# Chunked cross-attention on one core: softmax and value product in pieces of 512 tokens instead of 256, transposed squares placed by transfer alone

## The reference

```python
q, k, v = (ctx.transpose(0, 2, 1) @ W.T + b for W, b in ...)      # three 256 -> 256 projections of ctx
# tokens fall into chunks of 64; 8 heads of 32 channels
scores = einsum('bnqhd,bnkhd->bnhqk', q, k) / sqrt(32)            # 64 x 64 for each chunk and head
scores = scores + where(mask_of_key > 0, 0, -1e9)
out = einsum('bnhqk,bnkhd->bnqhd', softmax(scores), v)
out = (out @ W_out.T + b_out).transpose(0, 2, 1) * mask + x
return (out - mean(out, axis=2)) * rsqrt(var(out, axis=2) + 1e-5) # over the 2048 tokens of each channel
```

## Time and profile before

| | |
|---|---|
| median of 3 runs | 2021.92 us |
| the profiled execution: its own time / its span | 2024.09 / 2022.3 us |
| busy PE, PE weight loads, DVE, ACT, POOL | 97%, 79%, 87%, 77%, 74% of the span |
| share of PE in the chain that ended last | 96% |
| granted TensorE clock | 0.992 (mean; 1 is 2.4 GHz, 0.5 is 1.2 GHz) |

### The profile page before, as it was taken

How to read it: one execution, slowest core, us unless ns; L and a number is a source line. 1 busy time by engine, 2 the same in 40 slices (tenths; PEclk the granted TensorE clock), 3 DMA queues, 4 the chain that set the end, 5 groups by cost and what they waited for, 6 DMA issues and landing times.

```text
span 2022.3 us, 91553 instructions
## 1 busy us (share of the span) xinstructions
PE 1967.5 (97%) x40472; PEld 1597.4 (79%) x40472; DVE 1764.8 (87%) x2217; ACT 1565.7 (77%) x2176; POOL 1489.3 (74%) x1059
## 2 busy tenths in 40 slices
PE   7999999999999999999999999999999999999995
PEld 6888888777778888888878888888878778788883
DVE  5888988888888898888989889898889888888886
ACT  5778778777778877878777787777878778877773
POOL 4677777867777777777777777777776777777774
PEclk9999999999999999999999999999999999999997
DMA  4455666556665566665556666566655566655654
GB/s 157 128 160 174 169 187 181 166 147 169 181 179 165 161 173 181 186 180 168 163 173 184 172 177 173 165 171 187 180 163 160 171 177 177 170 172 165 173 147 146
DMA packets 242890, 342.55 MB, mean 169 GB/s; under 512 B 28992, under 2 KB 94784, under 8 KB 242496
## 3 DMA queue, kind: packets, MB, share of 16 engines
q1 hardware_dynamic: 242496, 336.71, 57.8%
HBM read 168.82 MB, written 67.11 MB: 117 GB/s over the span
## 4 chain that ended last, share of the span: by engine, by line
PE 96%; issue 2%; DVE 1%; POOL 0%; DMA 0%; ACT 0%; SPq 0%; DVEq 0%; POOLq 0%; ACTq 0%
PE proj_bank L308 38%; PE proj_bank L342 19%; PE proj_bank L365 18%; PE score_bank L383 11%; PE o_bank L416 10%; DMA b_cols<-b_in 0%; POOL y L590 0%; DVE row_max L658 0%; DVE stats L709 0%; DVE y L700 0%; POOL prob L572 0%; DVE w_lo L641 0%; DVE y L736 0%; DVE o_lo L689 0%; DVE prob L662 0%
## 5 line engine op out<-in xcount | busy, mean ns | idle before, releaser
L572 POOL TENSOR_TENSOR prob<-prob,recip 128x1024 f32<-128x1024 f32 x256 | 487.4, 1904 | 498.6 <-DVE recip L673 498.6
L658 DVE TENSOR_REDUCE row_max<-score_bank 128x16 f32<-128x1024 f32 x256 | 313.5, 1225 | 185.5 <-PE score_bank L383 181.8
L474 ACT ACTIVATE prob<-prob 128x1024 f32<-128x1024 f32 x256 | 271.6, 1061 | 235.2 <-DVE prob L662 235.2
L308 PE MATMUL proj_bank<-ctx_hi,w_hi 128*128 128x512 f32 x1024 | 349.2, 422 | 12.6 <-DVE ctx_lo L644 9.2
L580 POOL TENSOR_TENSOR ctx_lo<-ctx_raw,ctx_hi 128x512 fp32r<-128x512 f32 x255 | 329.6, 1293 | 18.2 <-ACT ctx_hi L454 18.2
L590 POOL TENSOR_TENSOR y<-y,x_raw 128x512 f32<-128x512 f32 x256 | 325.9, 1294 | 7.6 <-DVE y L700 7.5
L308 PE MATMUL proj_bank<-ctx_lo,w_hi 128*128 128x512 f32 x1024 | 322.6, 396 | 0.3 <-issue 0.3
L308 PE MATMUL proj_bank<-ctx_hi,w_lo 128*128 128x512 f32 x1024 | 319.9, 393 | 1.3 <-issue 1.3
L662 DVE TENSOR_TENSOR prob<-score_bank,row_max 128x1024 f32<-128x1024 f32 x256 | 313.4, 1224 | 8.8
L681 DVE STREAM_TRANSPOSE squares<-prob 128x1024 f32<-128x1024 f32 x256 | 315.8, 1234 | 1.5 <-POOL prob L572 1.5
L669 DVE TENSOR_REDUCE sums<-prob 128x16 f32<-128x1024 f32 x256 | 304.9, 1191 | 1.2 <-ACT prob L474 1.1
(11 more groups left out here) (46 smaller groups left out, 3691.9 us busy)
## 6 DMA issues: line engine op xcount, KB each, us to landing
ctx_raw<-ctx SPq DMA_DIRECT2D x128, 512.0 KB, 5.8
x_raw<-x SPq DMA_DIRECT2D x128, 512.0 KB
prob_t<-squares SPq DMA_DIRECT2D x1024, 64.0 KB, 2.5
out<-y SPq DMA_DIRECT2D x128, 512.0 KB, 6.9
mask_all<-mask SPq DMA_DIRECT2D x128, 256.0 KB, 4.2
v_x<-v_f SPq DMA_DIRECT2D x256, 128.0 KB, 3.5
y<-w_in_t SPq DMA_DIRECT2D x1, 768.0 KB, 5.7
y<-w_out_t SPq DMA_DIRECT2D x1, 256.0 KB, 6.7
```

Of the source, the lines that this page charges most:

```text
L308: last = pe.matmul(proj_bank[:, f, :], w[:, h, col + f * P:col + (f + 1) * P], c[:, n % 2, h, :], start=(a == 0 and h == 0), stop=(a == 2 ...
L572: pool.tensor_tensor(part, part, slots(recip[:, u % 2, :]), ALU.mult).then_inc(norm_done, 1)
L658: dve.tensor_reduce(row_max[:, :].rearrange("p (r c) -> p r c", c=CPU), rows, AX_X, ALU.max).then_inc(max_done, 1)
```

## The change

Every engine now walks over **periods** `p` of a whole block instead of units: `periods(step)` with `p` from -3 to 131. Scores, maximum, subtraction, transposition, `high_attention`, `low_attention` and value product handle 512 tokens in one piece. Exponentials, sums, division and `lay_negatives` are made in two instructions per block, split by heads (`half`), each as large as one of a unit before. `copy_squares` is gone; `move_probs` transfers all eight squares of a block. `squares` and `prob_t` have one buffer of double size. The masks have a ring of six. `rstd` and `shift` have two buffers.

The orders by period (PE, SP, DVE, ACT, POOL):

```diff
+            def step(p):                      # tensor
+                scores(p + 1)
+                project_k(p + 2, 0); project_k(p + 2, 1)
+                project_q(p + 2, 0); project_q(p + 2, 1)
+                project_out(p - 2, 0)
+                probs_times_v(p - 1)
+                project_out(p - 2, 1)
+                project_v(p + 2, 0); project_v(p + 2, 1)
+            def step(p):                      # sync
+                load_mask(p + 3); load_ctx(p + 6); load_x(p - 1)
+                move_values(p + 1); move_probs(p); store(p - 7)
+            def step(p):                      # vector
+                less_maximum(p + 1); turn(p); statistics(p - 3)
+                if done: mean_and_variance((p - 3) // BLOCKS)
+                output(p - 2, 0); sum_up(p + 1, 0)
+                output(p - 2, 1); sum_up(p + 1, 1)
+                reciprocals(p + 1); low_attention(p - 1)
+                if done: mean_shift((p - 3) // BLOCKS)
+            def step(p):                      # scalar
+                keys(p + 2, 0); split_ctx(p + 3, 0); keys(p + 2, 1); split_ctx(p + 3, 1)
+                queries(p + 2, 0); queries(p + 2, 1)
+                exponentials(p + 1, 0); exponentials(p + 1, 1)
+                lay_negatives(p + 2, 0); lay_negatives(p + 2, 1)
+                high_attention(p - 1)
+                values(p + 2, 0); normalise(p - 7); values(p + 2, 1)
+            def step(p):                      # gpsimd
+                low_ctx(p + 3, 0); low_ctx(p + 3, 1); masked_keys(p + 2)
+                normalise(p - 7); [reciprocal_std]
+                add_residual(p - 2, 0); add_residual(p - 2, 1)
+                divide(p + 1, 0); divide(p + 1, 1)
```

(The diff writes each call on a line of its own.) The core of the parts that changed inside:

```diff
             def move_probs(n):
+                sp.wait_ge(turned, n + 1)
+                wait(sp, pv_done, n)
                 for f in range(HALVES):
                     for a in range(2):
-                        b = 1 - a
+                        for b in range(2):
-                        sp.dma_start(prob_t[target, u % 2, a, :, :],
-                                     squares[source, u % 2, b, :, :]).then_inc(moved[u], 16)
+                            sp.dma_start(prob_t[target, a, :, :],
+                                         squares[source, b, :, :]).then_inc(moved[n % MOVES], 16)
...
             def turn(n):
                 dve.wait_ge(norm_done, 2 * (n + 1))
+                if there(n - 1):
+                    dve.wait_ge(moved[(n - 1) % MOVES], 128 * ((n - 1) // MOVES + 1))
...
             def project_v(n, f):
+                if there(n - 4):
+                    pe.wait_ge(y_done, 2 * (n - 4) + f + 1)
...
             def project_out(m, f):
+                if there(m + 4):
+                    pe.wait_ge(q_f_done, 2 * (m + 4) + f + 1)
```

More of the change, by code:

```diff
@@ L23 @@
 CPU = UNIT // CHUNK
+CPB = BLOCK // CHUNK
+ALL = BATCHES * BLOCKS
+MASKS = 6
+MOVES = 8
 SQ = 32
@@ L26 @@
 TPU = UNIT // P
[L27 removed]
+SLOTS = ROWS * CPB
 EPS = 1e-5
@@ L135, in attention_kernel @@
         turned = sem("turned")
-        squares_copied = sem("squares_copied")
-        moved = [sem(f"moved{u}") for u in range(UNITS)]
+        moved = [sem(f"moved{i}") for i in range(MOVES)]
         pv_done = sem("pv_done")
@@ L215, in store @@
             def store(n):
-                if not block_there(0, n):
+                if not there(n):
                     return
@@ L367, in project_out, with scores @@
                 last.then_inc(out_proj, 1)
-            def scores(B, u):
-                if not unit_there(B, u):
+            def scores(n):
+                if not there(n):
                     return
[L372 to L379, removed]
+                pe.wait_ge(q_f_done, 2 * (n + 1))
+                pe.wait_ge(k_f_done, 2 * (n + 1))
+                pe.wait_ge(seeded, 2 * (n + 1))
+                for c in range(CPB):
+                    tokens = slice(c * CHUNK, (c + 1) * CHUNK)
                     for r in range(ROWS):
@@ L407, in probs_times_v @@
                     pe.wait_ge(dve_const, 5)
-                wait(pe, o_lo_done, UPB * n + h)
-                pe.wait_ge(moved[u % UNITS], 64 * (n // BLOCKS + 1))
-                for c in range(CPU):
+                wait(pe, o_lo_done, n)
+                pe.wait_ge(moved[n % MOVES], 128 * (n // MOVES + 1))
+                for c in range(CPB):
                     for r in range(ROWS):
@@ L469, in exponentials @@
-            def exponentials(B, u):
-                if not unit_there(B, u):
+                if i == 0:
+                    act.wait_ge(neg_done, n + 1)
+                    if n == 0:
+                        act.wait_ge(opened, 1)
+                    wait(act, less_done, n)
+                act.activation(half(score_bank[:, :, :], i), neg_rows[:, n % 2, :].unsqueeze(1).broadcast_to(
+                    [P, ROWS // 2, BLOCK]), ACT.Copy).then_inc(seeded, 1)
+            def exponentials(n, i):
+                if not there(n):
@@ L494, in queries @@
-            def queries(B, n, f):
-                if not block_there(B, n):
-                    return
-                act.wait_ge(q_proj, count(B, 2 * BLOCKS, 2 * n + f + 1))
+                act.wait_ge(pv_done, m + 1)
+                wait(act, out_proj, 2 * (m - 1))
+                act.activation(o_hi[:, m % 2, :, :, :], o_block, ACT.Copy).then_inc(o_hi_done, 1)
+            def queries(n, f):
+                if not there(n):
+                    return
+                act.wait_ge(q_proj, 2 * n + f + 1)
@@ L675, in turn @@
[L675 to L681 removed]
+                dve.wait_ge(exp_done, 2 * n + i + 1)
+                dve.tensor_reduce(sums[:, i * SLOTS // 2:(i + 1) * SLOTS // 2], half(prob[:, n % 2, :, :, :], i).rearrange(
+                    "p r c k -> p (r c) k"), AX_X, ALU.add).then_inc(sums_done, 1)
@@ new lines, in reciprocals, with turn @@
+            def reciprocals(n):
+                if not there(n):
+                    return
+                wait(dve, norm_done, 2 * (n - 1))
+                dve.wait_ge(sums_done, 2 * (n + 1))
+                dve.reciprocal(recip[:, n % 2, :], sums[:, :]).then_inc(recip_done, 1)
+            def turn(n):
+                if not there(n):
+                    return
+                dve.wait_ge(norm_done, 2 * (n + 1))
+                if there(n - 1):
+                    dve.wait_ge(moved[(n - 1) % MOVES], 128 * ((n - 1) // MOVES + 1))
+                dve.transpose(squares[:, :, :, :], prob[:, n % 2, :, :, :].rearrange(
@@ L692, in output @@
-            def output(B, m, f):
-                if not block_there(B, m):
+                dve.wait_ge(o_hi_done, m + 1)
+                dve.tensor_tensor(o_lo[:, m % 2, :, :, :], o_block,
+                                  o_hi[:, m % 2, :, :, :].bitcast(F32), ALU.subtract).then_inc(o_lo_done, 1)
+            def output(m, f):
+                if not there(m):
                     return
-                dve.wait_ge(out_proj, count(B, 2 * BLOCKS, 2 * m + f + 1))
+                dve.wait_ge(out_proj, 2 * m + f + 1)
```

515 lines of the change are left out of this document (223 added, 292 removed).

## The result

The changed kernel takes 2098.28 us (median of 4, 2083.57 to 2109.33) against 2023.68 before: ratio 1.035, 95% interval [1.0314, 1.0387]. It is slower by 3.5%; 2004 was forecast, with 2045 as the upper end. The profiled execution took 2107.41 us, 83 more than the one before. Ratios and intervals leave out executions in the chip's slower state (one of e8_copy), medians do not.

A forecast was written before the change was run, and what follows sets the result against it. PE, 97% busy, was taken to bound the kernel. From 2024.1 us, -84 + 26 + 41 gave 2007, and with the profiled run 2.2 above the median, 2004 us; range 1985 to 2025, or 1964 to 2045 for 8 in 10.

The forecast's parts named there:

- Term 1: PE: merging small pieces saves 0.66 us a block, period 14.58 us, -84 us in all.
- Rival 4: PE: a seam inside merged pieces leaves only 0.20 us saved for each, 2038 us; chance 0.08.
- Term 2: DVE and projection bank: PE waits for the late output, worst every fourth period, +26 us.
- Rival 2: DVE and the projection bank set the period, at 15.0 us, 2011 us in all; chance 0.18.
- Term 3: PE's instruction stream: packets come late behind data, pauses 3.5 times the present ones, +41 us.
- rival 3: PE's instruction packets come late in every second block as merged pieces empty them in 1.5 us: 2061 us; chance 0.15.
- the same: Whole kernel: a change under 0.5% (10 us), which can't be told from none; chance 0.22.
- The squares and the single score bank: SP's eight square transfers and ACT's work before the next scores finish before PE needs them; costed at nothing.

The follow-up runs named there:

- e8_copy: Changed kernel with copy_squares back on ACT in two instructions, SP moving only the four off-diagonal squares, 67 MB less data: 2219.22 us, ratio 1.0922.
- e13: e10 with two useless transfers of 256 KB a block, issued apart, 67 MB in all: 1965.67 us, ratio 0.973.
- e1: Changed kernel with same transfers and bytes, but SP issues the loads and store apart, tied to halves of project_k and project_q: 2043.85 us, ratio 1.0102.
- e12: e10 with SP's order of the changed kernel, loads in one cluster behind the squares: 2148.88 us, ratio 1.0644.
- e5: Changed kernel with the value product moved ahead of both halves of project_out, so merged pieces stand evenly apart: 2028.94 us, ratio 1.0026.
- e14: e10 with the value product again between the halves of project_out, uneven distance: 1992.09 us, ratio 0.9845.
- e10: Changed kernel with squares copied on ACT (67 MB less), value product ahead of both project_out halves, loads issued apart at later points: 1951.29 us, ratio 0.9639.
- e9: Changed kernel with loads issued apart and the value product ahead of both project_out halves: 1997.42 us, ratio 0.9863.
- e3: Kernel before with one useless SBUF transfer of 256 KB in every unit, 67 MB in all, spread evenly: 2024.89 us, ratio 1.0004.
- e4: Kernel before with same bytes, but SP issues x, values, ctx and mask in one 1.5 MB cluster in even units: 2027.69 us, ratio 1.0019.

## Why the prediction was wrong, point by point

- **Term 1** (-84 us) was right: block of 14.59 us where nothing waits, and about -83 us. Both parts of it came: the large matmuls hold 11.65 us (11.58 forecast), the two pieces 2.94 (3.00). There is no seam in merged pieces: score pieces take 1.53 to 1.74, value pieces 1.42. Rival 4 falls.
- **Term 2** (+26) was about zero: in the waits PE waits for `output` twice, 5.7 us in all, in the emptying. I had the 2048-element instructions at 2.41 us; they took 2.29 (L631), and DVE waited 1.6 us a block for scores (209.1/128). Rival 2 falls.
- **Term 3** (+41) is the step that failed. The mechanism was named, and rival 3, priced at +97 and given 0.15, is what happened: +97 of idle PE. Its picture was near (64 pauses of 1.77 us against 53 of 1.88 on average between 60 and 1900); that the sums agree to 1 us is luck. I placed the value by the share of DMA and the mean room of a packet. What decides is neither mean: e13 has the share, 0.70, and loses 14 us. The runs show the cluster in SP's list (e1, e12) and the distance of the merged pieces (e5, e14); that the place of the cluster relative to the pieces counts is argued from e8. The share of the data queue itself was 73.4%, where some 69% were forecast. "SP also issues ... nearly without a break" stood in the prediction as half a sentence without a price.
- **A term was missing**, and so stood at nothing without a reason: behind a pause PE can go on at half clock. In the rows above the granted clock goes from 1.00 to 0.50 after PE stood still from 510.95, and `project_out` and `project_v` take nearly double for a while. That is +62 us. The Trainium skill, "TensorE: Matmul & The Clock Gate", section "What's actually happening", says that the throttled state is the default and activity releases it; the trace agrees. By this rule a pause can have a second price, though not every one had it (in e10 the clock fell behind one of 13). With it rival 3 would have been 2061 + 62 = 2123, and without the 26 us of term 2 it would have been 2097.
- **The chances**: rival 4 at 2038 lies above 2032, the upper end of "the same", so its 0.08 belonged to slower: 0.30 instead of 0.22.
- **The squares and the single score bank**, costed at nothing: right. PE waits for the squares' transfers for 3.0 us and for `lay_negatives` for 2.7 in the whole run.
- **The rule of the Trainium skill weighed in the prediction** ("Runtime: NRT & Kernel Launch", section "Instruction fetch mechanics": crossing a page of instructions is mostly hidden) agrees with the trace of e10 (idle PE 15.7) and not with that of the changed kernel (101.8). The Trainium skill, "DMA: Bandwidth & Descriptors", section "Queues, rings and completion order", says that each DMA engine goes round between queues packet by packet. By that rule a packet of instructions would pass a cluster after one packet of each queue; in the pause at 510.95 it began only when the data had nearly drained (2 data packets under way), 2.0 us after PE had stopped. But that is not the general case: in the pause at 614.61 it began at 615.12 with 15 data packets under way, and the median of the 53 is 13. So the traces don't show that a packet has to wait for a cluster to drain, and they don't contradict the rule.

How much of A and B there is in the changed kernel itself is known from undoing each alone there: -54 us for the cluster (e1), -69 for the distance (e5), -101 for both (e9). They overlap, which fits D, but doesn't prove it. Left open is by what the packet is held up: the trace shows the time at which it begins, not the time at which it was asked for. It does show how short the room is. Of the packets between 60 and 1900 us none began more than 278 instructions ahead of the place at which PE stops for want of it (296 in the kernel before), and a merged piece is 256 instructions in 1.5 us.

## What to carry to other kernels

When instructions on the bottleneck engine are packed more densely, its stream of instructions becomes a load with a due time: look for "issue" inside runs that have no wait, and at the DMA share just before. Issue large loads apart, tied to points of the bottleneck engine's own work, not one behind another; it was worth 54 us in the changed kernel and 198 in the variant that copies the squares, at even distance. Where two dense runs of instructions can't be avoided, set them at equal distances (69 us here). Price a pause of some microseconds on TensorE with the half clock behind it.

## What the runs showed of the hardware

- The same 67 MB more cost nothing with pieces of 64 matmuls (e3, 1.0004) and 14 us with merged ones (e13).
- The same cluster order cost 198 us with merged pieces at a mean DMA share of 0.60 (e12), while a cluster of 1.5 MB with pieces of 64 cost 4 us (e4). A mean share of DMA says little about late instructions.
- Less data went with a kernel slower by 121 us (e8 against the changed kernel); in its rows the cluster lies right ahead of a merged piece.
- All 53 gaps of PE over 0.45 us in the changed kernel, and all 13 in the kernel before, stand at the same place in the count of instructions modulo 256 (behind the 193rd to 195th of 256) and end 1.2 to 1.7 us after a packet of instructions of 16 KB, which takes 0.9 to 2.8 us, 1.1 as a median.
- The DVE maximum over 2048 elements from PSUM took 2.292 us where two of 1024 took 2.450 (2 x 1.225).
